# A hand-ordered attention and MLP kernel on one core: later loads, two score banks for the first image, and separate places for the first and last images

## The reference

```python
xn = layer_norm(x)                        # then padded from 16x16 to windows of 14x14
qkv = win @ qkv_w + qkv_b                 # 12 heads of 16 channels
attn = einsum('bqc,bkc->bqk', q * scale, k)
attn = attn + rel_h[..., None] + rel_w[..., None, :]   # q against the relative tables, rows and columns
out = softmax(attn) @ v
x = shortcut + (out @ proj_w + proj_b)    # windows put back, cut to 16x16
x = x + (gelu(layer_norm(x) @ fc1_w + fc1_b) @ fc2_w + fc2_b)
```

## Time and profile before

| | |
|---|---|
| median of 3 runs | 537.08 us (535.59 to 541.04) |
| profiled execution | 536.93 us, span of the core 535.1 us |
| PE (matmul) busy | 508.8 us, 95% |
| DVE busy | 390.6 us, 73% |
| ACT busy | 265.5 us, 50% |
| POOL busy | 135.8 us, 25% |

### The profile page before, as it was taken

How to read it: one execution, slowest core, us unless ns; L and a number is a source line. 1 busy time by engine, 2 the same in 40 slices (tenths; PEclk the granted TensorE clock), 3 DMA queues, 4 the chain that set the end, 5 groups by cost and what they waited for, 6 DMA issues and landing times.

```text
span 535.1 us, 12318 instructions
## 1 busy us (share of the span) xinstructions
PE 508.8 (95%) x4554; PEld 461.9 (86%) x4554; DVE 390.6 (73%) x924; ACT 265.5 (50%) x526; POOL 135.8 (25%) x318
## 2 busy tenths in 40 slices
PE   7999889999999999999999999999999999998847
PEld 7988767899898998999898999998989989777737
DVE  5247966978888888878888888888797877764230
ACT  2130424555655565634555564655555555564712
POOL 1202312323032323213232323223232312230210
PEclk9779977999999999989999999999999999999998
DMA  6853142241414040400404040403122130402000
GB/s 173 262 147 99 47 128 61 77 135 44 121 46 143 2 142 3 128 17 11 134 2 143 1 141 5 129 16 113 32 75 70 37 108 2 143 2 92 0 16 15
DMA packets 29759, 40.98 MB, mean 77 GB/s; under 512 B 5795, under 2 KB 14467, under 8 KB 29699
## 3 DMA queue, kind: packets, MB, share of 16 engines
q1 hardware_dynamic: 29699, 40.20, 25.8%
HBM read 6.57 MB, written 1.57 MB: 15 GB/s over the span
## 4 chain that ended last, share of the span: by engine, by line
PE 88%; DVE 4%; issue 3%; ACT 3%; DMA 1%; POOL 1%; DVEq 0%; ACTq 0%; POOLq 0%; SPq 0%
PE back L820 16%; PE back L1046 12%; PE by_query L971 9%; PE by_key L986 9%; PE times_v L996 9%; PE front_b L820 7%; PE front_b L937 6%; PE front_a L937 6%; PE front_a L820 4%; PE back L1012 2%; PE back L1019 1%; PE front_a L869 1%; PE times_v L854 1%; PE back L869 1%; DMA q_stack<-rel_lo 1%
## 5 line engine op out<-in xcount | busy, mean ns | idle before, releaser
L759 DVE TENSOR_REDUCE row_max<-by_query 128x2 f32<-128x512 f32 x192 | 131.9, 687 | 50.7 <-PE by_query L971 49.3
L529 ACT ACTIVATE probs<-by_key 128x512 f32<-128x512 f32 x192 | 110.5, 596 | 78.0 <-PE by_key L986 71.8
L971 PE MATMUL by_query<-k_stack,q_stack 108*128 108x256 f32 x384 | 84.9, 303 | 4.3 <-DVE row_max L759 3.3
L986 PE MATMUL by_key<-q_stack,k_stack 110*128 110x256 f32 x384 | 80.4, 306 | 2.3 <-ACT probs L529 2.3
L971 PEld LDWEIGHTS by_query<-k_stack,q_stack 108*128 108x128 f32 x384 | 60.1, 194 | 13.8 <-issue 8.3
L1046 PE MATMUL back<-w,hid 128*128 128x192 f32 x384 | 69.6, 326 | 0.0
L986 PEld LDWEIGHTS by_key<-q_stack,k_stack 110*128 110x128 f32 x384 | 56.8, 190 | 10.3 <-issue 6.2
L1046 PEld LDWEIGHTS back<-w,hid 128*128 128x128 f32 x384 | 61.6, 190 | 0.3
L820 PE MATMUL back<-xn_hi,w_hi 128*128 128x256 f32 x192 | 53.9, 291 | 1.8 <-DVE xn_hi L668 1.6
L820 PE MATMUL back<-xn_hi,w_lo 128*128 128x256 f32 x192 | 53.3, 288 | 0.0
L996 PE MATMUL times_v<-probs,v_ones 128*32 128x256 f32 x768 | 53.1, 395 | 0.0
(11 more groups left out here) (135 smaller groups left out, 986.1 us busy)
## 6 DMA issues: line engine op xcount, KB each, us to landing
q_stack<-q_hi SPq DMA_DIRECT2D x32, 192.0 KB, 2.7
k_stack<-k_hi SPq DMA_DIRECT2D x32, 192.0 KB, 3.1
q_stack<-rel_hi SPq DMA_DIRECT2D x32, 168.0 KB
q_stack<-rel_lo SPq DMA_DIRECT2D x32, 168.0 KB
q_stack<-q_lo SPq DMA_DIRECT2D x16, 192.0 KB, 3.1
k_stack<-k_lo SPq DMA_DIRECT2D x16, 192.0 KB, 3.1
X<-in_x SPq DMA_DIRECT2D x8, 192.0 KB, 7.5
k_stack<-av_t SPq DMA_DIRECT2D x8, 192.0 KB
```

The costliest lines, as they stand in the source:

```text
L529: act.activation(probs[h % NP], KB[h % 2][:, :].rearrange("p (k t) -> p k t", k=2), ACT.Exp).then_inc(s_ex, 1)
L759: dve.tensor_reduce(row_max[:, h, :], QB[:, :].rearrange("p (a t) -> p a t", a=TILES), AX, ALU.max).then_inc(s_smax, 1)
L971: last = pe.matmul(QB[:, a * TOK:(a + 1) * TOK], q_stack[n % 2][0:ROWS_Q, h, a * P:(a + 1) * P], k_stack[n % 2][0:ROWS_Q, h, :], start=Tru ...
L986: last = pe.matmul(KB[h % 2][:, c * TOK:(c + 1) * TOK], k_stack[n % 2][0:ROWS_K, h, c * P:(c + 1) * P], q_stack[n % 2][0:ROWS_K, h, :], st ...
```

## The change

PLACE becomes five tables, each with own places for an even and an odd n: one for n = 0 and 1, one for n = 2 and 3, one for n = 4 to 11, one for n = 12 and 13, one for n = 14 and 15. The numbers are finer by ten; PERIOD is now that of a pair. The loads of images 2 to 7 and of the layer's weights get places of their own. The dummy matmuls become a step `fill` of 2 each, with 24 places, all for the first image, in the bank by_key1 instead of times_v. For n = 0 the odd heads of `by_query` write the bank times_v (which is not used before `times_v` of image 0), and `by_query` waits for the maxima of head h-2.

The numbers sorted, the first orders are these (n.part). SP after the constant rows of buffer 0: `load_images` 2; `stack_k` 0.0, `stack_q` 0.1, 0.0, `stack_rel` 0.0, 0.2, 0.3, `stack_k` 0.1, `stack_rel` 0.1; then `load_back(0)`, the constant rows of buffer 1, `load_images` 3, `load_mlp(0)`, `scatter_pads` 0, the stacks of image 1 and so on, with image 4 behind the stacks of image 2, 5 behind those of image 3, 6 and 7 near those of images 4 and 5. POOL, image 0: `rel_high` 0.0, 0.1, `take_pads` 0 (before: 0.0, `take_pads`, 0.1). DVE: both `rel_low` of image 0 ahead of `pads_max`.

```diff
-PERIOD = 44970
-PLACE = {
-    "load_images": (464046,), "stack_k": (939000, 941616), "stack_q": (923758, 930529),
-    "stack_rel": (924570, 939951, 944132, 950403), "load_rest": (950573, 710986, 548006, 1008948),
...
+PERIOD = 899400
+TABLES = (
+    {
+        "load_images": ((8606000,), (9055700,)),
+        "stack_k": ((8164724, 9285597), (9622863, 9619921)),
+        "stack_q": ((8986097, 8424887), (9889561, 9619193)),
+        "stack_rel": ((8997228, 9294067, 9234621, 9234621), (9608561, 9856604, 9846927, 9921145)),
+        "load_rest": ((9353616, 9436246, 9331139, 10089480), (9955430, 7559560, 5929760, 9923400)),
...
+        "take_pads": ((8004340,), (8776339,)),
...
+        "back_products": ((8759864, 9421710), (8967720, 9871410)),
...
+def table(pair):
+    return TABLES[pair if pair < 2 else pair - N2 // 2 + len(TABLES) if pair >= N2 // 2 - 2 else 2]
 def in_order(*steps):
-    turns = [(n * PERIOD + at, i, n, part) for i, step in enumerate(steps)
-             for part, at in enumerate(PLACE[step.__name__]) for n in range(N2)]
+    turns = [(pair * PERIOD + at, i, 2 * pair + odd, part) for i, step in enumerate(steps)
+             for pair in range(N2 // 2) for odd, places in enumerate(table(pair)[step.__name__])
+             for part, at in enumerate(places)]
...
+        def scores(n, h):
+            return VB if n == 0 and h % 2 else QB
...
-                dve.tensor_reduce(row_max[:, h, :], QB[:, :].rearrange("p (a t) -> p a t", a=TILES), AX,
+                dve.tensor_reduce(row_max[:, h, :], scores(n, h)[:, :].rearrange("p (a t) -> p a t", a=TILES), AX,
                                   ALU.max).then_inc(s_smax, 1)
...
-            def keep_busy(count):
-                for _ in range(count):
-                    pe.matmul(VB[:, 0:P], blank[:, :], blank[:, :], start=True, stop=True)
+            def fill(n, part):
+                if part == 0:
+                    pe.wait_ge(s_blank, 1)
+                for _ in range(2):
+                    pe.matmul(KB[1][:, 0:P], blank[:, :], blank[:, :], start=True, stop=True)
...
-                else:
-                    if n == 0:
-                        keep_busy(2)
+                elif n > 0:
                     pe.wait_ge(s_smax, HEADS * n + h)
+                elif h > 1:
+                    pe.wait_ge(s_smax, h - 1)
                 for a in range(TILES):
-                    last = pe.matmul(QB[:, a * TOK:(a + 1) * TOK], q_stack[n % 2][0:ROWS_Q, h, a * P:(a + 1) * P],
+                    last = pe.matmul(scores(n, h)[:, a * TOK:(a + 1) * TOK], q_stack[n % 2][0:ROWS_Q, h, a * P:(a + 1) * P],
                                      k_stack[n % 2][0:ROWS_Q, h, :], start=True, stop=True)
```

More of the change, by code:

```diff
@@ L52 @@
 FRONT_AT, BACK_AT = (0, 2), (0, 5)
-PERIOD = 44970
-PLACE = {
-    "load_images": (464046,), "stack_k": (939000, 941616), "stack_q": (923758, 930529),
-    "stack_rel": (924570, 939951, 944132, 950403), "load_rest": (950573, 710986, 548006, 1008948),
-    "scatter_pads": (966784,), "stack_top": (995617, 1004667), "store": (1353193,), "root0": (779627,),
-    "q_high": (825092,), "rel_high": (835970, 848736), "take_pads": (843901,), "pads_combine": (856135,),
-    "pads_shift": (862916,), "pads_weigh": (869516,), "pad_arguments": (912429,), "pad_sums": (915010,),
-    "add_proj_bias": (952813,), "root1": (959936,), "add_fc2_bias": (982464,), "front_weights": (159783, 1004531),
-    "high0": (867597,), "q_out": (870419,), "k_out": (870427,), "rel_h_out": (906742,), "pads_exp": (914737,),
-    "pads_exp2": (923065,), "neg_top_high": (959333,),
-    "exps": (960401, 969623, 970091, 970920, 975064, 975704, 983032, 987938, 997671, 998000, 1002146, 1002570),
-    "pad_factors": (975462,), "back_weights": (919416, 960059), "att_out": (1011006,), "high1": (1042860,),
-    "gelus": (1046168,), "front_rest": (809189, 956237), "stats0": (774943,), "hat0": (799232,), "low0": (813131,),
-    "k_low": (828782,), "v_out": (832734,), "q_low": (843379,), "rel_w_out": (851749,), "rel_low": (852982, 856699),
-    "pads_max": (854721,), "pads_shifted": (855261,), "pads_sum": (869032,), "pads_top": (871610,),
-    "row_maxima": (871113, 871887, 876415, 879781, 885597, 889029, 896454, 897021, 898926, 900107, 900428, 902467),
-    "pads_total": (883896,), "tops": (902832,), "neg_top_low": (903307,), "times_v_out": (939869, 944673, 955699),
-    "back_rest": (927186, 958326), "normalise": (961495,), "after_attention": (966946,), "stats1": (973382,),
-    "hat1": (975904,), "low1": (986645,), "after_mlp": (994599,), "front_products": (253467, 942155),
-    "transpose0": (801236,), "q_products": (808096,), "k_products": (811728,), "v_products": (815208,),
-    "rel_products": (819789, 825323, 831509, 837041), "pad_products": (840639,),
-    "by_query": (853257, 856932, 860745, 862872, 868891, 874692, 877890, 884646, 885124, 887137, 888076, 891548),
-    "top_transposes": (893762,),
-    "by_key": (902439, 903172, 905781, 906402, 908697, 910789, 917251, 918290, 921546, 926248, 927277, 927536),
-    "times_v": (917180, 932065, 941067), "back_products": (851802, 942171), "to_tokens": (944976,),
-    "att_transposes": (947902,), "projection": (951070,), "transpose1": (966617,), "fc1": (974907, 975125, 978011),
-    "fc2": (979882, 980726, 981708, 981887, 984617, 985130),
-}
@@ L893, in q_products @@
                 l = n // IMAGES
-                if n == 0:
-                    keep_busy(6)
                 pe.wait_ge(n_lo[0], n + 1)
@@ L943, in pad_products @@
                 l = n // IMAGES
-                if n == 0:
-                    keep_busy(8)
                 pe.wait_ge(s_rc, n + 1)
@@ L1049, in fc2 @@
                     last.then_inc(s_f2, 1)
-            for step, n, part in in_order(front_products, back_products, transpose0, transpose1, q_products, k_products, v_products, rel_products,
+            for step, n, part in in_order(fill, front_products, back_products, transpose0, transpose1, q_products, k_products, v_products, rel_products,
                                           pad_products, by_query, top_transposes, by_key, times_v, to_tokens, att_transposes,
```

446 lines of the change are left out of this document (440 added, 6 removed).

## The result

| | before | after |
|---|---|---|
| median | 536.34 us (4 executions) | 551.56 us (4 executions) |
| ratio, 95% interval | | 1.0291 (1.0230 to 1.0353) |
| profiled execution, span | 535.1 us | 549.5 us |
| mean granted clock | 0.965 | 0.947 |

The change makes the kernel 2.9% slower; 535.8 us was forecast. (Ratios leave disturbed executions out and the medians of the experiments don't, so the two need not agree to the last tenth.)

What follows compares the result with a forecast made beforehand. TensorE was taken as full in the middle, so only start and drain could gain. Against the profiled 536.93: +1.4 (image 0 with bias products) - 1.8 (image 1) - 0.7 (drain) = -1.1, so 535.8 us; range 530.0 to 541.5.

Steps and rivals of the forecast that it cites:

- Later loads: Start: later image and weight loads and earlier rel_high bring image 0's first score to 31.3 instead of 34.75, 3.4 us earlier.
- whose chain is not earlier: Start: image 1's transpose0 waits for the pads, taken as no earlier, and ends at 28.5, ahead of q_products.
- Image 0's scores: Two banks and an earlier first score: tops of image 0 end near 55.0 instead of 56.04, lead 0.9 to 2.6.
- R1.3: Image 0, a part of R forecast to end near 46.7; the chain behind it to tops was put at 8.3 us.
- The bias products: Moved ahead of image 1's scores: 6.9 us instead of 3.8 from tops to k_products' end; lag of 1.4 taken.
- I let the two cancel: Start: up to 1.7 us lost to half clock at 56 to 60, set against 1.7 gained if none at 32.1.
- Image 1's scores: Work fills TensorE's gap at 72; tops of image 1 end at 78.8 to 79.9 instead of 81.24; gain 1.8 taken.
- The steady part: Middle images: TensorE is full and swaps cost nothing unless something becomes late; zero, bounds +1 and -6.
- The drain: Last images: pads_sum ahead of the last times_v_out shortens the path to image 15's first maxima; 0.7 gained, bounds 0 and 1.4.
- The second: Start: bias products pull the clock down before image 1's scores, nothing won at 32.1; 540.4 us, chance 0.14.
- The first: Start: clock stays up, neither 32.1 to 38.9 nor 73 to 86.6 slow; 6.2 gained, 530.7 us, chance 0.24.
- The third: Steady part: odd images' first score waits for its last stack, seven images losing 0.9 us each; 543 us, chance 0.10.

Runs made afterwards that it cites:

- bias_moved: Kernel before with one step moved, the first layer's bias products behind top_transposes 0: 543.92 us, ratio 1.0126.
- start_bias_back: New order for images 0 to 3 only, with load_back, load_mlp and the bias products ahead as before: 541.54 us, ratio 1.0107 to the kernel before.
- start_only: Kernel before with the changed kernel's order for images 0 to 3 alone (new loads, banks and fills): 541.00 us, ratio 1.0075.
- start_spread: New start alone, bias products in seven pieces between image 0's last scores replacing three fills, load_mlp behind load_back: 537.92 us, ratio 0.9999 to the kernel before.
- middle_only: Kernel before with the changed order of all engines for images 4 to 12 alone: 542.34 us, ratio 1.0103.

## Why the prediction was wrong

- **What bounds the kernel** held: no instruction was removed, and the middle was full. But "busy" in the earlier trace rows was read as if it meant that the clock was safe, and an order without slack was read as one that can only be improved.
- **Later loads.** Right in kind: the stack is no longer what the first score waits for (stack DMAs land in 2.7 to 3.6 us), `q_products` is. 31.3 was forecast, 33.31 measured. The step that failed is "whose chain is not earlier" with the cast "some 1.2 us before 24.93": the pads' chain came later. `take_pads` started at 25.94 and not at 23.78, since its `rel_full` came 1.3 us later and the cast now stands ahead of it and took 1.01 us (from 24.98) and not 0.61. Alone, the loads are worth 0.4% (0.16% lost to 0.94% won).
- **Image 0's scores.** `tops` at 51.35, where 55.0 was taken and 53 to 55 named: the half clock of 32.1 to 38.9 did not come. A lead of 4.5 instead of 0.9 to 2.6. In the changed kernel neither the products nor a DMA wait stood there; bias_moved, with the wait and without the products, had it. (Behind R1.3 the listed terms add up to 8.0, not 8.3.)
- **The bias products.** Place and sign right, the size wrong: 6.48 us for 3.6, and the two front products behind them at half clock, so 11.2 from the end of `tops` to that of `k_products` for 6.9. The end at 62.7 was forecast at 60 to 62; a lag of 2.9 where 1.4 was taken. The step that failed is "I let the two cancel": the half clock under and behind the products cost 2.9 + 1.1 us, not 1.7. Its cause was not the forecast one either: it fell 0.1 us ahead of the products, and in start_bias_back without them. No step of the prediction asked what the clock would do in the wait ahead of `tops` 0.
- **Image 1's scores.** Forecast 1.8 gained, measured 2.1 lost from `tops` 1 to 2: the half clock at about 79 to 89 us came all the same, with `tops` 1 at 82.03 and not 78.8 to 79.9. The step from `tops` 1 to 2 is as long in start_only, start_bias_back and start_spread (31.7 to 31.8 us); nothing was run to find out why.
- **The steady part**, taken as zero with bounds +1 and -6: 4.9 us in the trace, 1.03% by middle_only. The step that failed looked at TensorE's order only, and at VectorE's mean share (4 of 25 us free); of what stood ahead of each maximum, and what GpSimd did beside it, nothing was worked out. The bound of -6 held, the value of zero didn't.
- **The drain**, taken as 0.7 gained, cost 6.3 us, of which 4.6 hang on the two adds and 1.7 are not explained. The two adds of GpSimd were in the diff, and the trace of before has VectorE's `rel_lo` at 1.89 us where its sister takes 0.68; no step asked which operations would now run side by side.
- **Rivals.** The second had its sign, a stretch at 0.50 in front of image 1's scores, but its mechanism only in part: in bias_moved the clock fell behind the products, in the changed kernel ahead of them. It stopped at 540.4, because it was put on top of a sum with two zeros. The first was half right (no half clock from 28 to 50) and still lost. The third's wait came at image 12 alone, in two of the experiments and not in the changed kernel.

## What to carry to other kernels

When an order written out by hand changes on several engines, price each engine's order on its own: for each step of the busiest chain, what now stands ahead of it on the engine that serves it (here VectorE), and what runs beside that on GpSimd. A mean share of free time says nothing about it. And matmuls of one column are not harmless fillers: ten blocks of them cost 41 us more than wide ones, in the clock of the work behind them. Where TensorE waits anyway, as in the kernel before, their own time is hidden, though the clock fell behind them there as well (at 32.09).

## What the runs showed of the hardware

**TensorE's clock falls behind busy one-column matmuls.** Ten of ten blocks of 24 were followed by half clock, none of ten with 112 columns, with TensorE busy without a gap from each block's start to 5 us later. The Trainium skill, "TensorE: Matmul & The Clock Gate", Part 1, puts the clock down to how busy TensorE has recently been; by the busy share of the profile the trace doesn't agree for these blocks, and the measurement decides. It agrees in kind at 50.00 in start_bias_back, where the clock fell behind 2 us with 1.17 busy.

**VectorE and GpSimd stop each other.** Beside 0.61 + 1.01 + 1.01 us of GpSimd, one `xhat` operation took 2.66 us instead of 0.37; `rel_lo` took 0.68 alone and 1.89 to 2.44 beside such operations; the maxima, which read PSUM, kept their 0.68. It goes the other way too: in the trace of the kernel before, the cast `rel_hi`, 0.61 us alone, took 1.07 beside `rel_lo`:

```profile
310.96 1.89 DVE L713 TENSOR_TENSOR rel_lo<-rel_full,rel_hi 84x512 fp32r<-84x512 f32 x1
...
311.30 1.00 POOL L429 TENSOR_TENSOR X<-X,b 128x384 f32<-128x384 f32 x1
...
312.25 1.07 POOL L366 CAST rel_hi<-rel_full 84x512 fp32r<-84x512 f32 x1
```

The Trainium skill, "SBUF — State Buffer", section "SBUF: two separate sides", says that the two engines share one pair of ports as an exclusive lock, which a VectorE operation in a two-port mode, or with two SBUF inputs beside a GpSimd operation that reads SBUF, needs, and that the loser waits for the whole instruction. The trace agrees with that rule, as the 2.66 us end 0.12 us behind GpSimd's last add; in which mode `xhat` ran it does not show.
